# Eight-block network on one core: three reorderings, at the encoder's layer seam, in its feed-forward and in the linear attention

## The reference

```python
# block 1: six encoder layers, 16 sequences of 256 tokens, 16 heads of width 8
for l in range(6):
    a = softmax(mask(q @ k.T / sqrt(8))) @ v          # q, k, v = x @ Wq + bq, ...
    x = ln(x + a @ Wo + bo) * g1 + b1
    h = gelu(x @ W1 + b1)                             # 128 -> 512
    x = ln(x + h @ W2 + b2) * g2 + b2
# block 5: linear attention with cumulated sums
qf, kf = elu(q) + 1, elu(k) + 1
num = einsum(qf, cumsum(kf * v)); den = einsum(qf, cumsum(kf)) + 1e-6
y = ln(x + (num / den) @ Wo + bo) * gamma + beta
```

## Time and profile before

| | |
|---|---|
| median of three runs | 4416.31 us |
| the profiled execution | 4428.41 us, of it 4426.6 us span |
| TensorE busy | 83% of the span |
| VectorE busy | 60% |
| ScalarE busy | 41% |
| GpSimd busy | 21% |
| encoder | 0 to 2035 us of the span |
| linear attention | 3458 to 3690 us |

### The profile page before, as it was taken

One profiled execution on the slowest core, in us unless ns is written; L12 is line 12 of the kernel. 1 busy time (PEld: TensorE's weight loads), 2 busy tenths in 40 slices (PEclk: granted clock), 3 DMA queues, 4 the chain that ended last, 5 costly groups with the idle time before them and its releaser, 6 DMA issues. The chain is left out here.

```text
span 4426.6 us, 70777 instructions
## 1 busy us (share of the span) xinstructions
PE 3675.6 (83%) x27255; PEld 2541.7 (57%) x27255; DVE 2640.8 (60%) x6733; ACT 1825.8 (41%) x2861; POOL 910.5 (21%) x1164
## 2 busy tenths in 40 slices
PE   5998998997998998985999978677756666997996
PEld 3665665665665666664777745455535433443664
DVE  5866866866867857854222239888668562113663
ACT  2553554553554554552333335322223122331443
POOL 2323333333333333321000001000100230003321
PEclk8998999998998998997999987799867677997996
DMA  5414514414514524501000000000000000003430
GB/s 135 117 45 113 116 45 116 116 40 109 120 43 104 125 48 102 120 27 44 1 1 1 1 15 1 0 1 1 1 6 1 4 0 27 0 0 82 97 84 24
DMA packets 156741, 225.01 MB, mean 51 GB/s; under 512 B 16159, under 2 KB 136351, under 8 KB 139423
## 3 DMA queue, kind: packets, MB, share of 16 engines
q10 hardware_dynamic: 19656, 107.37, 11.1%
q1 hardware_dynamic: 136750, 113.11, 9.3%
HBM read 156.84 MB, written 60.82 MB: 49 GB/s over the span
## 5 line engine op out<-in xcount | busy, mean ns | idle before, releaser
L781 DVE TENSOR_REDUCE enc_mx<-psum 128x2 f32<-128x512 f32 (+1 forms) x1152 | 755.6, 684 | 184.0 <-PE psum L490 181.1
L963 ACT ACTIVATE enc_e<-psum 128x1024 f32<-128x1024 f32 (+1 forms) x768 | 580.2, 808 | 423.4 <-PE psum L511 341.6
L490 PE MATMUL psum<-enc_ks,enc_qs 80*128 80x128 bf16 (+1 forms) x3072 | 460.5, 253 | 63.5 <-DVE enc_mx L781 51.5
L511 PE MATMUL psum<-enc_qs,enc_ks 83*128 83x256 bf16 (+1 forms) x3072 | 382.8, 250 | 47.1 <-DMA enc_qs<-enc_turned_max 41.3
L490 PEld LDWEIGHTS psum<-enc_ks,enc_qs 80*128 80x128 bf16 x3072 | 222.5, 100 | 201.1 <-DVE enc_mx L781 101.5
L522 PE MATMUL psum<-enc_e,enc_v 128*32 128x256 f32 (+1 forms) x6144 | 332.5, 334 | 0.0
L511 PEld LDWEIGHTS psum<-enc_qs,enc_ks 83*128 83x128 bf16 x3072 | 259.9, 99 | 85.9 <-DMA enc_qs<-enc_turned_max 42.1
L1832 ACT ACTIVATE moe_act_h<-psum 128x512 f32<-128x512 f32 x288 | 169.2, 598 | 306.1 <-PE psum L1706 305.8
L1728 PEld LDWEIGHTS psum<-par_s,moe_act_h 128*128 128x128 f32 x2304 | 269.7, 192 | 30.1 <-issue 28.5
L1795 DVE SCALAR_TENSOR_TENSOR moe_acc<-psum,moe_gates,moe_acc 128x128 f32<-128x128 f32 x256 | 72.0, 344 | 345.4 <-PE psum L1728 345.4
L1728 PE MATMUL psum<-par_s,moe_act_h 128*128 128x128 f32 x2304 | 272.6, 275 | 0.0
(11 more groups left out here) (473 smaller groups left out, 7056.8 us busy)
## 6 DMA issues: line engine op xcount, KB each, us to landing
enc_qs<-q_pieces ACTq DMA_DIRECT2D x234, 192.0 KB
enc_ks<-k_pieces ACTq DMA_DIRECT2D x234, 192.0 KB
k_pieces<-enc_pieces SPq DMA_DIRECT2D x240, 128.0 KB, 2.0
q_pieces<-enc_pieces SPq DMA_DIRECT2D x144, 128.0 KB, 2.1
enc_qs<-q_pieces SPq DMA_DIRECT2D x54, 192.0 KB
enc_ks<-k_pieces SPq DMA_DIRECT2D x54, 192.0 KB
rope_qs<-q_pieces ACTq DMA_DIRECT2D x39, 192.0 KB
rope_ks<-k_pieces ACTq DMA_DIRECT2D x39, 192.0 KB
```

The source lines that it names most:

```text
L490: last = T_.matmul(p1[f % 2][:, i * kw:(i + 1) * kw], qs[0:KEYED, slot, h, j * P:(j + 1) * P], ks[0:KEYED, slot, h, 0:kw], start=True, sto ...
L511: last = T_.matmul(p2[ch][:, g], ks[0:SCORED, slot, 4 * T + g, ch * P:(ch + 1) * P], qs[0:SCORED, slot, 4 * T + g, 0:n], start=True, stop= ...
L781: V.tensor_reduce(mx[:, u % 2, j * HEADS + h0:j * HEADS + h0 + n], p1[f % 2].rearrange("p (h k) -> p h k", h=n), AX_X, ALU.max)\
L963: A.activation(e_of(T, ch), p2[ch], ACT.Exp, scale=HD ** -0.5).then_inc(s_e, 1)
```

## The change

In the encoder, `layerr`'s load goes into the next layer's list of SyncE, behind the second sequence's `row_of_maxima` and ahead of the stores of group 2. The turn and `back2` of group 7 go behind the first scores (ScalarE: behind `expo(0, 0)`), and the first sequence's third fill goes ahead of its projection. In the feed-forward of all layers but the last, the turn of group `g` goes from behind `down(g + 1)` to behind the second of four products of `up(g + 3)`; the turn of group 6 goes between the last six fills. VectorE's wait for a turn goes from ahead of the statistics to ahead of `apply`. In the linear attention, `project` runs one slot further ahead, behind the last sums; the features go ahead of `N2.statistics`, and the exponentials ahead of `N2.move`.

```diff
@@ -316,14 +316,15 @@
                 for u in range(SEQS):
                     if u + 1 < SEQS:
                         row_of_maxima(layer, 0, u + 1)
+                    if u == 0 and layer:
+                        sp.wait_ge(N2.s_done, layer * GROUPS + GROUPS)
+                        sp.wait_ge(s_res2, layer * GROUPS + GROUPS)
+                        sp.dma_start(LR.sb[:], c.params["layerr"][1:][ds(layer - 1, 1)].rearrange("l p w -> p (l w)")).then_inc(LR.sem, 16)
                     if u % 2 == 0 and u // 2 + 2 < GROUPS:
                         store(layer, 0, u // 2 + 2)
                 if not last:
                     sp.dma_start(LQ.sb[:], c.params["layerq"][1:][ds(layer, 1)].rearrange("l p w -> p (l w)")).then_inc(LQ.sem, 16)
                     first(layer, 1)
-                    sp.wait_ge(N2.s_done, at(layer, GROUPS, 2 * GROUPS))
-                    sp.wait_ge(s_res2, at(layer, GROUPS, 2 * GROUPS))
-                    sp.dma_start(LR.sb[:], c.params["layerr"][1:][ds(layer, 1)].rearrange("l p w -> p (l w)")).then_inc(LR.sem, 16)
 
             first(0, 0)
             for layer in range(LAYERS - 1):
@@ -613,6 +614,10 @@
                         pe.wait_ge(N4.s_done, g)
                     N4.turn(pe, g, bank[1])
 
+            def last_turn(layer):
+                pe.wait_ge(N2.s_done, at(layer, GROUPS, 2 * GROUPS - 1))
+                N2.turn(pe, at(layer, GROUPS, GROUPS - 1), misc)
+
             def attend(layer, last_layer):
                 for u in range(SEQS):
                     m, odd = u // 2, u % 2
@@ -622,6 +627,10 @@
                         fills(0)
                         scores_t(layer, u, T, 1)
                         fills(1)
+                        if T == 0 and u == 0:
+                            if layer:
+                                last_turn(layer - 1)
+                            fills(2)
                         if T == 0 and not odd and m + 2 < GROUPS:
                             if m >= 2:
                                 pe.wait_ge(N1.s_done, at(layer, GROUPS, m - 1))
@@ -654,7 +663,8 @@
                             values(layer, u, T - 1)
                         elif u:
                             values(layer, u - 1, 3)
-                        fills(2)
+                        if T or u:
+                            fills(2)
                         if T == 0 and not odd:
                             if m + 2 < GROUPS:
                                 pe.wait_ge(s_rest, at(layer, 2 * GROUPS, 2 * (m + 2) + 1))
@@ -678,15 +688,29 @@
                                     pe.wait_ge(s_masked, at(layer, SEQS, u + 1))
                                 N1.turn(pe, at(layer, GROUPS, m - 1), misc)
                 values(layer, SEQS - 1, 3)
+                def turn_rows(g):
+                    if g == 0:
+                        pe.wait_ge(N1.s_done, at(layer, GROUPS, GROUPS - 1))
+                    elif g == 6 and not last_layer:
+                        pe.wait_ge(s_nmm, at(layer, SEQS, 1, 1))
+                    else:
+                        pe.wait_ge(N2.s_done, at(layer, GROUPS, GROUPS + g))
+                    N2.turn(pe, at(layer, GROUPS, g), misc)
+
                 up(layer, 0)
                 turn_sums(layer, SEQS - 1, 1)
                 for g in range(GROUPS):
                     behind = (lambda f: fill(layer, 1, (g - 5) // 2, 6 * ((g - 5) % 2) + f) if f < 3 else None) if g >= 5 and not last_layer else (lambda f: None)
+                    def after(f):
+                        if f == 1 and g >= 2 and not last_layer:
+                            turn_rows(g - 2)
+                        behind(f)
+
                     if g + 1 < GROUPS:
-                        up(layer, g + 1, behind)
+                        up(layer, g + 1, after)
                     else:
                         for f in range(3):
-                            behind(f)
+                            after(f)
                     if g == 0:
                         turn_att(layer, GROUPS - 1, bank[0])
                     if g == 1:
@@ -703,14 +727,8 @@
                         pe.wait_ge(N2.s_done, at(layer, GROUPS, GROUPS + 6))
                         turn_max(layer, 1, 0)
                     down(layer, g, among)
-                    if g:
-                        if g == 1:
-                            pe.wait_ge(N1.s_done, at(layer, GROUPS, GROUPS - 1))
-                        elif g == 7 and not last_layer:
-                            pe.wait_ge(s_nmm, at(layer, SEQS, 1, 1))
-                        else:
-                            pe.wait_ge(N2.s_done, at(layer, GROUPS, GROUPS + g - 1))
-                        N2.turn(pe, at(layer, GROUPS, g - 1), misc)
+                    if g and last_layer:
+                        turn_rows(g - 1)
                     if g == 2:
                         pe.wait_ge(s_att_tm, at(layer, GROUPS, GROUPS))
                         N1.turn(pe, at(layer, GROUPS, GROUPS - 1), bank[0])
@@ -721,11 +739,13 @@
                     if last_layer:
                         close(g)
                 if not last_layer:
-                    for f in range(6, 12):
+                    for f in range(6, 9):
                         fill(layer, 1, 1, f)
-                pe.wait_ge(N2.s_done, at(layer, GROUPS, 2 * GROUPS - 1))
-                N2.turn(pe, at(layer, GROUPS, GROUPS - 1), misc)
+                    turn_rows(GROUPS - 2)
+                    for f in range(9, 12):
+                        fill(layer, 1, 1, f)
                 if last_layer:
+                    last_turn(layer)
                     for k in range(GROUPS, GROUPS + 5):
                         close(k)
 
@@ -877,8 +897,6 @@
                 for g in range(1, GROUPS + 1):
                     n = at(layer, GROUPS, g - 1)
                     go_on = not last
-                    if g > 1:
-                        dve.wait_ge(N2.s_turned, n)
                     if g == 1:
                         add2(layer, 0)
                     N2.statistics(dve, n)
@@ -894,6 +912,8 @@
                         u, f0 = ((0, 3), (0, 9), (1, 3), (1, 9))[g - 5]
                         for f in range(f0, f0 + 3):
                             reduce(layer, 1, u, f)
+                    if g > 1:
+                        dve.wait_ge(N2.s_turned, n)
                     if n and not last:
                         dve.wait_ge(s_scaled2, n)
                     elif n:
@@ -1008,6 +1028,8 @@
                     m, odd = u // 2, u % 2
                     for T in range(HT):
                         expo(layer, u, T)
+                        if u == 0 and T == 0 and layer:
+                            back2(layer - 1, GROUPS - 1)
                         if T < 2 and not odd and m + 2 < GROUPS:
                             high(layer, 0, m + 2, T, misc)
                         if T == 0 and odd and m:
@@ -1050,8 +1072,8 @@
                             high(layer, 1, 1, w, bank[w])
                     if last:
                         close(g)
-                back2(layer, GROUPS - 1)
                 if last:
+                    back2(layer, GROUPS - 1)
                     for k in range(GROUPS, GROUPS + 5):
                         close(k)
 
@@ -2244,6 +2266,7 @@
             pe.wait_ge(s_w, 5)
             pe.wait_ge(s_ones, 1)
             pe.wait_ge(s_bias, 16)
+            project(0)
             for k in SLOTS_K:
                 if 0 <= k - 1 < GROUPS:
                     g = k - 1
@@ -2253,8 +2276,6 @@
                     for t in range(TILES):
                         last = T_.transpose(bank[6][:, t * P:(t + 1) * P], att[:, t, :], c.ident)
                     last.then_inc(s_att_t, 1)
-                if 0 <= k + 1 < GROUPS:
-                    project(k + 1)
                 if 0 <= k - 1 < GROUPS:
                     g = k - 1
                     pe.wait_ge(s_att_tm, g + 1)
@@ -2279,6 +2300,8 @@
                 if 0 <= k + 1 < GROUPS:
                     sums(k + 1, 2)
                     sums(k + 1, 3)
+                if 0 <= k + 2 < GROUPS:
+                    project(k + 2)
                 if 0 <= k - 1 < GROUPS:
                     g = k - 1
                     if g:
@@ -2366,10 +2389,10 @@
                 if now:
                     products(k, 0)
                     reduce(k, 0)
+                if 0 <= k + 1 < GROUPS:
+                    features(k + 1)
                 if 0 <= k - 2 < GROUPS:
                     N2.statistics(dve, k - 2)
-                if 0 <= k + 1 < GROUPS:
-                    features(k + 1)
                 if now:
                     products(k, 1)
                     reduce(k, 1)
@@ -2401,15 +2424,6 @@
                     if k:
                         act.wait_ge(s_p3, k)
                     A.activation(last_sums[:], bank[5][:, 0:PAIR], ACT.Copy).then_inc(s_last, 1)
-                if 0 <= k - 2 < GROUPS:
-                    if k - 2:
-                        act.wait_ge(N2.s_normed, k - 2)
```

(15 more changed lines are left out.)

## The result

| | before | after |
|---|---|---|
| median, 11 runs each | 4421.0 us (4411.0 to 4429.7) | 4405.4 us (4396.0 to 4422.9) |
| ratio to before | | 0.9967, 95% interval 0.9956 to 0.9978 |
| span of the profiled execution | 4426.6 us | 4402.3 us |

The change makes the kernel 15.6 us faster by the medians, 0.33% by the ratio. The forecast was 43 us (4373 us, range 4340 to 4403). The two profiled executions differ by 24.3 us.

What follows compares the result with a forecast made beforehand. TensorE was taken to carry the encoder, and its loop to set the linear attention's slot. 5 x (3.0 seam + 5.5 feed-forward) = 42.5, and 1 from the linear attention: about 43 us, 4373 us; range for 8 in 10, 4340 to 4403.

Steps and rivals of the forecast that it cites:

- Both old waits: Encoder, TensorE: waits for normalised rows ahead of a turn, 72.1 us, and for the row of maxima, 34.1 us.
- the new stall: Seam, second sequence: TensorE waits 3.9 us for the exponential at the third pair of scores, in place of 5.84.
- the slot stayed near 24 us: Linear attention: sign of a right forecast, a slot stays near 24 us; 19 us would show rival B.
- the distance between two weights' issues: Encoder: sign of a right forecast, this distance falls by about 8.5 us.
- The feed-forward, 5.5 us a layer: Feed-forward of five layers: moved turns remove waits, 2.1 + 1.9 + 1.0 + 0.4 + 0.1 us; bounds 2.5 and 7.
- The wait predicted there, 2.6 us for the turn of group 3: Feed-forward, middle of up(6): TensorE stands about 2.6 us because the root of group 3 ends no sooner.
- The seam, second sequence, 1.9 us: Seam: the row of maxima's 5.84 us stall goes, a 3.9 us stall replaces it; gain 2.4 to loss 0.4.
- the loads' release: Seam, second sequence: ScalarE's loads go 7.4 us after the release, when weights and stores have landed; bounds 6.9 and 9.7.
- The seam, first sequence, 1.1 us: Seam: the projection starts at about 389.7 instead of 390.84; gain 1.1 us, bounds 0 (clock rises later) and 2.7.
- The upper bound for both sequences: Seam, first and second sequence together: gain 3.0 us, bounds -0.4 and 7.
- The linear attention, -1: Linear attention: the projection leaves one place in TensorE's loop and returns ahead of N1.turn; net -1 us, -8.6 to +9.
- Rival C: Feed-forward bound by GpSimd's cuts and roots, waits come back whole; 20 us gained, 4396 us; 22% with other shortfalls.

Runs made afterwards that it cites:

- e6: Changed kernel with half the bytes in the six loads for the next layer's first sequence, layers 1 to 5; 4400.7 us, ratio to before 0.9947.
- e7: Changed kernel with group 3's turn and the first fills behind the fourth product of up(6), fills 2 to 5 among down(5); 4390.0 us, ratio to before 0.992.
- e3: Kernel before with only the feed-forward's turns moved among the next group's products; 4416.3 us, ratio 0.9979.
- e1: Kernel before with only the weights' load placed behind the second sequence's row of maxima; 4419.0 us, ratio 0.9996.
- e5: Changed kernel with the eight stores of group 2 ahead of the weights in SyncE's list; 4396.0 us, ratio to before 0.9935.
- e13: e11 plus four products per seam that nobody reads, placed in TensorE's short waits; 4330.0 us, ratio 0.9779.
- e14: e12 plus six products per seam that nobody reads, three ahead of the turn at its old place; 4323.7 us, ratio 0.9766.
- e8: Changed kernel with N1.turn ahead of the projection in the linear attention; 4389.1 us, ratio to before 0.9924.
- e2: Kernel before with only group 7's turn and back2 moved behind the next layer's first scores; 4435.3 us, ratio 1.0027.
- e10: e9 with turn and back2 of group 7 put back to the layer's end; 4387.5 us, ratio to before 0.9918.
- e16: Changed kernel with turn and back2 of group 7 back at the layer's end; 4410.6 us, ratio 0.9964.
- e4: Kernel before with only the linear attention's part of the change; 4423.2 us, ratio 0.9998.
- e15: Kernel before with both seam edits, weights and last turn, feed-forward and linear attention as before; 4431.0 us, ratio 1.0003.
- e9: Changed kernel with group 2's stores right behind the second sequence's row of maxima and the weights behind the third's; 4387.5 us, ratio to before 0.9918.
- e11: Changed kernel with the edits of e7, e8 and e9 together; 4347.2 us, ratio 0.9822.
- e12: e11 with turn and back2 of group 7 at the layer's end; 4334.8 us, ratio 0.9797.

## Why the prediction was wrong

**Right in kind.** Both old waits went for the most part, and the new stall is where it was put: at the third pair of scores, behind ScalarE's queued loads, with half clock behind it. The turns of the feed-forward stopped waiting but for one. VectorE's wait in the linear attention became others, and the slot stayed near 24 us (its first turn begins at 3555.11, 3579.28 and 3602.90). But the distance between two weights' issues, which was to fall by 8.5 us, fell from 325.9 to 323.5 us, mean of four.

**The feed-forward, 5.5 us a layer: the step that failed.** The sum followed TensorE, ScalarE, VectorE and GpSimd through the moved turns, but not the load of the next layer's first sequence. In the kernel before no row shows a wait for it, only its slack (SyncE's and TensorE's rows of the first seam before):

```profile
341.17 0.33 SPq L275 DMA_DIRECT2D enc_qs<-q_pieces  x1
...
352.39 0.39 PE L490 MATMUL psum<-enc_ks,enc_qs 80*128 80x256 bf16 x2
```

The first fill stood 11.2 us behind the first issue. The load needs 9.2 us (341.65 to 350.86 after), so 2.0 us were to spare. In the changed kernel TensorE would start the fill at 346.72 (350.86 less 4.14), only 5.1 us behind the issue. The wait predicted there, 2.6 us for the turn of group 3, is real (2.10 in e6), but hidden under 4.14 us for the load. Measured: 1.1 us a layer by the segments, 21 to 22 us short over five. With half the load 4.2 a layer were there (e6), and with other work in the gap 4.6 (e7), so the other terms of the 5.5 held for the most part. My own trace reading after the result, 3 us, was also too high: e3 gave 0.8 alone.

**The seam, second sequence, 1.9 us.** The mechanism was right, and a term was mis-sized: the loads' release. I read the pair's end off a window of the DMA's work (7.4 us); the loads went 9.46 us after the release at 404.55, near the upper bound of 9.7. In windows of 0.25 us the pair's last bytes of before move until 411.75, 7.9 us behind the weights' issue. In after the bulk is through at 412.75, 8.1 us behind it, but a DMA share of 0.07, at 20 to 23 GB/s, goes on to 413.50, and the loads go at 414.01. e1 has the same tail (0.07 and 20 GB/s up to 412.25, the loads at 412.72). The term took the end of the bulk for the landing. The stall was 5.99, not 3.9. Of the second sequence's gain of 2.6 us, the third took 1.4 back in half clock. Net 1.2 (e1: nothing). The Trainium skill says that each DMA engine takes the descriptors of a ring in order ("DMA: Bandwidth & Descriptors", Queues, rings and completion order). That stores issued behind the weights are held up by them follows from it, and e5 agrees in direction, with 3.3 us. The estimate from the same page of the Trainium skill (Bandwidth: 6.15 us for 1 MB, measured for transfers issued from GpSimd), 5.9 us in full and a landing at 12.4, was too much; the trace has 5.4 us from the weights' issue to their landing, and 9.46 us to the loads. The prediction gave the rule too little weight where it took 7.4.

**The seam, first sequence, 1.1 us.** The projection did come 1.07 us sooner behind the turn. It brought nothing: 27.5 against 27.1 us. The bound 0 was named with its reason, that the clock rises later when the work is in two pieces, and a later rise is what the rows show: 1.91 us for a product at 396.18, where the same product of before, at 396.33, took 1.02. That the two pieces are the reason isn't shown: e3, which leaves the last turn where it was, has a first sequence of 28.3 us, too. e13 and e14 show that this sequence paid about 3 us for the clock, far more than the turn's place could win. About 1.5 us a seam short, 7 us in all. That the edit of the feed-forward would lengthen the half clock at the seam was no term of the sum. (The upper bound for both sequences adds up to 7.7, not 7; nothing hangs on it.)

**The linear attention, -1.** 3.5 to 4.6 us gained in the traces, inside the bounds; the loop was the right one (e8), and the forecast put the projection at 4.4 us a piece where it took 3.5 (3570.93 to 3574.40), since it ran partly at full clock.

Together, 43 less 21.5 (feed-forward), 7 and 3.5 (seam), and 3.6 more for the linear attention is 15, and 15.6 were measured. So close a match is luck in part. Of the 24.3 us between the two profiled executions 11.2 lie ahead of the encoder's end and 4.6 in the linear attention; 8.5 lie in stages that the change doesn't touch. Rival C had the nearest time, 4396 us, but for another reason: GpSimd's cuts and roots didn't bind, a load did. The range let the feed-forward fall to 2.5 us a layer and the seams to -0.4, but not both together, though both hung on transfers of whose landing the kernel before showed no wait.

**What stays open.** Why the last turn alone cost 12 us in e2, while its place makes no difference in e10 and e16. The traces show where most of it goes. The table has the first sequence's segment and TensorE's time at half clock, counted in windows of 1 us over the 30 us from 2 us ahead of each layer's first marker, both as means over the five seams and over the kernels named:

| | last turn at its old place | last turn moved |
|---|---|---|
| feed-forward's old order | before, e1, e4: 26.7 us, 12.1 us at half clock | e2, e15: 28.5, 18.1 |
| feed-forward changed | e3, e10, e16: 27.9, 15.5 | after, e5, e8, e9: 27.9, 17.3 |

With the old feed-forward the moved turn costs 1.8 us a seam, 9 us in all, and goes with 6 us more at half clock. The changed feed-forward costs 1.2 us a seam by itself, about what it gains in its own segment, and then the turn's place adds nothing. Why the clock falls for longer in these orders no run shows; e13 and e14 show only that filling the waits ends it.

## What to carry to other kernels

When waits are taken from one engine, list every transfer that was just in time in the old profile: a load that shows no wait may have little slack, and can be the next bound. What stood next behind the weights on their queue was late in each of three places tried: the row in before (5.84 us), the stores in after (5.99 us), the third row in e5 (2.45 us). So put the large transfer where the next small one is far away (here behind the third row). Before moving work to fill a stall, ask what the clock does: here dummy products in four to six short waits won more than the moved turn, and the orders chosen from the profile of the change (e14) took the kernel from 4428.0 to 4323.7 us, 2.3% below before and 2.0% below the change by the ratios.

## What the runs showed of the hardware

- Short waits alone can cost the clock. At the first seam of e11, waits of 1.90, 1.60, 1.34, 0.44 and 1.56 us with work between them went with a granted clock of 0.50 from about 377 to 393 us, and in before, where one wait is 3.46 us, it was 0.50 from 382 to 392. With four fillers (e13) it fell only between 385 and 389 us, and with six (e14) it was 1.00 throughout this seam.
- The six transfers of 192 KB for one sequence, issued within 2.3 us (341.65 to 344), landed 9.2 us after the first issue, with six more and then stores queued behind them, at 160 to 205 GB/s in total. With half the bytes they landed 5.6 us after it (338.90 to 344.5).
- A stage whose code no variant touched isn't constant between programs: the rope block took 264 us from its first to its last reduction in e1, e4 and e12, and 267 to 275 in the others. So differences of up to some 10 us between two programs can't be put down to the edit without a trace that shows the place.
